# The exponentials of a softmax taken head by head from PSUM on ScalarE, in a kernel of attention, sampling and two recurrences

## What is computed

```python
xn = _rms_norm(x, g_norm) * (1.0 + scale) + shift
q, k, v = ...(xn @ W_qkv)                     # 16 heads, d = 32
q = _rms_norm(q, g_q)
k = _rms_norm(k, g_k)
logits = jnp.einsum('bhqd,bhkd->bhqk', q, k) * d ** (-0.5)
attn = jax.nn.softmax(logits, axis=-1)
o = jnp.einsum('bhqk,bhkd->bhqd', attn, v)
x = x + o + o @ W_out
```

## Time and profile before

| | |
|---|---|
| median of 3 runs | 1828.99 us (1824.32 to 1829.84) |
| profiled execution | 1831.36 us, span 1829.4 us |
| TensorE, matmuls, busy | 1593.6 us (87%) |
| VectorE busy | 1582.0 us (86%) |
| ScalarE busy | 821.4 us (45%) |
| GpSimd busy | 697.0 us (38%) |
| mean granted clock of TensorE | 0.967 |

### The profile page before, as it was taken

The page is one execution under the profiler, slowest core; times in us unless marked ns, Lnnn a source line. Parts: engine busy times, 40 slices in busy tenths (PEclk is TensorE's granted clock), DMA queues, the critical chain, the costliest instruction groups (busy, mean ns, idle before and its releaser), DMA issues.

```text
span 1829.4 us, 100329 instructions
## 1 busy us (share of the span) xinstructions
PE 1593.6 (87%) x44506; PEld 1398.0 (76%) x44506; DVE 1582.0 (86%) x3935; ACT 821.4 (45%) x1886; POOL 697.0 (38%) x832
## 2 busy tenths in 40 slices
PE   5778778788878787885799999999999999999995
PEld 4355555556555555555799999999999999999995
DVE  5699999999999999986289888888988988899887
ACT  3533333323333333333255555555555555555553
POOL 2333333333333333334433444434443344434342
PEclk9889999999999999997799999999999999999999
DMA  5200010000000000002000000000000000000000
GB/s 183 93 16 23 25 25 18 24 23 25 26 25 17 25 23 26 20 13 80 6 10 14 13 14 16 14 13 14 13 15 15 13 13 15 15 14 13 14 15 15
DMA packets 91905, 45.47 MB, mean 25 GB/s; under 512 B 75984, under 2 KB 84240, under 8 KB 91472
## 3 DMA queue, kind: packets, MB, share of 16 engines
q1 hardware_dynamic: 91024, 39.03, 8.9%
q0 software_dynamic: 448, 0.02, 0.1%
HBM read 30.56 MB, written 8.45 MB: 21 GB/s over the span
## 4 chain that ended last, share of the span: by engine, by line
PE 49%; DVE 1%; issue 1%; POOL 0%; ACT 0%; POOLq 0%; ACTq 0%; DVEq 0%
PE ps_RZ L1032 20%; PE ps_F L1059 13%; PE ps_N L1032 10%; PE ps_F L1064 6%; DVE ps_S L1199 0%; DVE rest L1199 0%; DVE ts L1224 0%; DVE cub L1228 0%; ACT ps_T L1096 0%; POOL en L1337 0%; DVE ps_E L1199 0%; DVE qst L1199 0%; DVE Qs L1323 0%; DVE Hf L1220 0%; DVE P L1316 0%
## 5 line engine op out<-in xcount | busy, mean ns | idle before, releaser
L1059 PE MATMUL ps_F<-ts,Cp 128*128 128x64 f16 x8192 | 283.2, 193 | 12.7 <-ACT ts L1096 11.5
L825 PE MATMUL psQ<-Wx,front 128*128 128x512 f16 x1152 | 285.6, 401 | 1.2 <-issue 1.2
L1059 PEld LDWEIGHTS ps_F<-ts,Cp 128*128 128x128 f16 x8192 | 257.5, 98 | 14.6 <-ACT ts L1096 12.4
L634 DVE TENSOR_SCALAR E<-rows,lidx 128x512 f16<-128x512 f16 x512 | 229.4, 500 | 0.0
L1096 ACT ACTIVATE ts<-qst 128x256 f16<-128x256 f32 x192 | 80.1, 417 | 311.1 <-DVE qst L1199 311.1
L825 PEld LDWEIGHTS psQ<-Wx,front 128*128 128x128 f16 x1152 | 115.7, 103 | 133.7 <-issue 29.6
L1032 PE MATMUL ps_RZ<-xs,Wx 128*128 128x64 f16 x6144 | 204.0, 194 | 3.8 <-POOL xs L1341 2.4
L1032 PE MATMUL ps_RZ<-hs,Whh 128*128 128x64 f16 x6144 | 201.6, 193 | 1.3 <-POOL hs L1337 0.4
L1032 PEld LDWEIGHTS ps_RZ<-xs,Wx 128*128 128x128 f16 x6144 | 191.0, 99 | 5.5 <-POOL xs L1341 2.9
L1032 PEld LDWEIGHTS ps_RZ<-hs,Whh 128*128 128x128 f16 x6144 | 188.5, 98 | 2.4 <-issue 1.6
L1064 PE MATMUL ps_F<-ts,Cp 128*128 128x64 f16 x4096 | 163.0, 193 | 1.0 <-issue 0.3
(11 more groups left out here) (167 smaller groups left out, 3515.3 us busy)
## 6 DMA issues: line engine op xcount, KB each, us to landing
front<-in_x SPq DMA_DIRECT2D x32, 256.0 KB, 3.6
rows<-rows_dram SPq DMA_DIRECT2D x64, 128.0 KB, 3.0
out<-ot SPq DMA_DIRECT2D x512, 16.0 KB, 1.8
XR<-in_L_cond_W_qkv SPq DMA_DIRECT2D x4, 768.0 KB, 16.3
E<-in_L_cond_W_hh SPq DMA_DIRECT2D x4, 768.0 KB, 4.4
front<-in_L_cond_W_ih SPq DMA_DIRECT2D x4, 768.0 KB, 5.8
XR<-in_L_cond_W_emb SPq DMA_DIRECT2D x1, 2048.0 KB, 11.0
E<-in_L_cond_coupling SPq DMA_DIRECT2D x1, 1024.0 KB, 5.5
```

The lines of the kernel that those rows point to most:

```text
L634: e = v.tensor_scalar(E[b][:, t, c, :], rows[b][:, :], lidx[:, t, c:c + 1], None, ALU.is_equal)
L825: last = mm(psQ[:, n, :], xn[p.u][:, i, c, :], Wqkv[:, j, c, n * D:(n + 1) * D], start=(c == 0 and t == 0), stop=(c == KC - 1 and t == 2))
L1059: mm(psF[:, s % 2, m, :], Cp[:, i, c, m * PART:(m + 1) * PART], ts_[:, 0, c, :], start=(c == 0 and m == 0 and i == 0), stop=False, skip_gr ...
```

## The change

`subtract_max` becomes `least`: VectorE takes the minimum of each head (`mn`) straight from the scores, which now carry the opposite sign, as `gqk` is negated. ScalarE computes exp(-score + minimum) from `psS` for each of the 16 heads in an instruction of its own, with the minimum as bias and the sum over the head written to `den` by `accum_out`. `sum_p` becomes `invert_sum`, the reciprocal alone. The waits of `turn_qk`, `scores` and `turn_x` for `sub_done` become waits for `exp_done`.

```diff
-        v.tensor_scalar(gqk[:, :], gq[:, 0:1], gq[:, 1:2], float(DH) ** -0.5, ALU.mult, ALU.mult)
+        v.tensor_scalar(gqk[:, :], gq[:, 0:1], gq[:, 1:2], -float(DH) ** -0.5, ALU.mult, ALU.mult)
...
         def exps(p):
-            act.wait_ge(sub_done, p.n + 1)
-            a(S[:, :, :], S[:, :, :], ACT.Exp).then_inc(exp_done, 1)
+            act.wait_ge(mn_done, p.n + 1)
+            need(act, p_T, p.n)
+            need(act, rden_done, p.n)
+            for c in range(4):
+                for r in range(4):
+                    h = c * 4 + r
+                    last = a(S[:, h, :], psS[:, r, c * T:(c + 1) * T], ACT.Exp, scale=-1.0, bias=mn[:, r, c:c + 1],
+                             accum_out=den[:, h:h + 1])
+            last.then_inc(exp_done, 1)
...
-        def subtract_max(p):
-            sc = psS[:, :, 0:256].rearrange("p r (c k) -> p r c k", c=4)
+        def least(p):
             dve.wait_ge(sc_done, p.n + 1)
-            v.tensor_reduce(mx[:, :, :], sc, AX.X, ALU.max).then_inc(mx_done, 1)
-            dve.wait_ge(mx_done, p.n + 1)
-            need(dve, p_T, p.n)
-            v.tensor_tensor(S[:, :, :].rearrange("p (c r) k -> p r c k", r=4), sc,
-                            mx[:, :, :].unsqueeze(3).broadcast_to([PART, 4, 4, T]), ALU.subtract).then_inc(sub_done, 1)
+            need(dve, exp_done, p.n)
+            v.tensor_reduce(mn[:, :, :], psS[:, :, 0:256].rearrange("p r (c k) -> p r c k", c=4), AX.X, ALU.min).then_inc(mn_done, 1)
...
-        def sum_p(p):
+        def invert_sum(p):
             dve.wait_ge(exp_done, p.n + 1)
-            v.tensor_reduce(den[:, :], S[:, :, :], AX.X, ALU.add).then_inc(den_done, 1)
-            dve.wait_ge(den_done, p.n + 1)
             need(dve, p_done, p.n)
             v.reciprocal(rden[:, :], den[:, :]).then_inc(rden_done, 1)
...
         def turn_x(p):
             pe.wait_ge(y_done, p.n + 1)
             pe.wait_ge(x_in[p.u], p.half * 16 + 16)
-            need(pe, sub_done, p.n - 2)
+            need(pe, exp_done, p.n - 2)
```

More of the change, by code:

```diff
@@ L298, in attention_and_sampling @@
     S = sb("S", [PART, HEADS, T])
-    mx = sb("mx", [PART, 4, 4])
+    mn = sb("mn", [PART, 4, 4])
     den = sb("den", [PART, HEADS])
@@ L331, in attention_and_sampling @@
     qk_T, qk_hi, qk_ready = sem("qk_T"), sem("qk_hi"), sem("qk_ready")
-    sc_done, mx_done, sub_done, exp_done = sem("sc_done"), sem("mx_done"), sem("sub_done"), sem("exp_done")
-    den_done, rden_done, p_done = sem("den_done"), sem("rden_done"), sem("p_done")
+    sc_done, mn_done, exp_done = sem("sc_done"), sem("mn_done"), sem("exp_done")
+    rden_done, p_done = sem("rden_done"), sem("p_done")
     p_T, pt_hi, pt_ready = sem("p_T"), sem("pt_hi"), sem("pt_ready")
@@ L764, in slot @@
             if p := pair(-1):
-                subtract_max(p)
+                least(p)
             if tap:
@@ L768, in slot @@
             if p := pair(-1):
-                sum_p(p)
+                invert_sum(p)
             if tap:
@@ L799, in turn_qk @@
             pe.wait_ge(qn_done, p.n * 2 + 2)
-            need(pe, sub_done, p.n)
+            need(pe, exp_done, p.n)
             need(pe, pt_ready, p.n)
```

## The result

The changed kernel takes 1874.5 us (median of 4 runs, 1869.5 to 1879.7) against 1827.4 for the kernel before: ratio 1.026, 95% interval 1.0225 to 1.0292. It is slower by 47 us; 62 were forecast. Its profiled execution has a span of 1877.9 us, 48.5 more than that of before.

A forecast was written before the change was run, and what follows sets the result against it. VectorE was taken to bound the attention and sampling slots, TensorE the recurrences. Longer slots (46.8 + 3.9 = 50.7 us) plus clock falls (11.5) gave 62.2 us on the 1829.0 median: 1891 us, range 1855 to 1940.

The forecast's parts named there:

- Who sets the slot: VectorE in the attention and sampling slots: almost no slack, so its path from maximum to second tap product sets their length.
- The price of a head: ScalarE's sixteen exponentials: 0.31 us a head for ACTIVATE and accumulator read, 5.08 us in all in place of 1.06.
- Rival A: ScalarE's accumulator reads run in series: 0.42 to 0.53 us a head, kernel about 1932 to 1990 us; chance 0.2.
- rival B: Small ScalarE instructions overlap fully: 0.12 us a head, about 1784 us; chance 0.04 faster, 0.03 time unchanged near 0.22.
- The segment: VectorE from reduction to second tap product: 5.02 to 6.53 us, 1.51 more a slot, 46.8 us over 31 slots.
- The slot of pair 0: Slot in which nothing is sampled or projected out: the delay of `turn_x` lacks cover, costing 3.9 us instead of 1.5.
- The clock: TensorE idles longer before `turn_p`, so its granted clock falls in ten more slots, 1.15 us each: 11.5 us.
- The total: Whole kernel: 50.7 us of longer slots plus 11.5 us of clock falls, 62.2 us slower; chance of slower 0.92.

## Why the prediction was right, and where its sizes were off

*Who sets the slot.* Right. VectorE's order from the reduction to the second tap product is the slot: 5.02 to 6.29 us there, 24.66 to 25.92 us in the slot. That the wait and not ScalarE's load is the loss is shown by the new order: -122 us with the same instructions, of which VectorE's idle time is the larger part (83 of the 104 us over 24 slots).

*The price of a head.* 0.31 us were forecast from rows of 512 elements, 0.29 measured; the sixteen 4.85 instead of 5.08 us. The rows gave the pointer as 0.099 and the read as 0.10; taken away one by one they are 0.094 and 0.09. Rival A (reads in series, 0.42 and more) and B (full overlap, 0.12) are both excluded. The pitch of 0.22 us at which rival B was to decide doesn't go with its 3.57 us for all: by the prediction's own 15 pitches and the 0.43 of the last pair it is 0.21.

*The segment.* 1.27 us more a slot, 1.51 forecast: 0.23 by the heads. Over the 30 slots behind that of pair 0 up to the last reduction this is 38 us, where the sum has 46.8 for 31; it is the largest part of the miss.

*The slot of pair 0.* +5.0, forecast 3.9. `turn_x` is released by the exponentials and the projection behind it ran at the lower clock:

```profile
80.16 1.94 PE L914 MATMUL psS<-ident,front 128*128 128x128 f32 x8 [9.56 <-issue]
...
81.89 4.88 PE L826 MATMUL psQ<-Wx,front 128*128 128x512 f16 x12
...
86.81 0.60 ACT L486 ACTIVATE front<-psQ 128x512 f32<-128x512 f32 x1 [0.83 <-PE psQ L826]
```

In the earlier trace rows ScalarE was ready for the squares only at 84.99 because of its copies; now it waits for TensorE.

*The clock.* Size right (13.6 us, 11.5 forecast; 12 more long slots, ten forecast; 1.15 us each), its ground wrong. The forecast had `turn_x` all but unmoved and the gap in front of `turn_p` longer by 1.5 us. That gap stayed (2.47 us on average before, 2.35 after). The 0.3 us were taken from the slot of the earlier trace rows, in which `turn_x` starts 6.0 us after the reduction; in 20 of the 27 slots it starts 4.4 to 5.1 us after, as in the slot from 373.99 (378.62). Moved to 6.3 us it opens a new gap of up to 1.6 us, and `project(p, 0)` behind it moves as well, which is why the gap in front of `turn_p` doesn't grow. So TensorE's waits in a slot did grow by about 1 us (from 2.5 to (51.6 + 23.9) / 22 = 3.4), but in another place. That idle time brings on the falls is shown by the filled kernels for the gap in front of `turn_p`. That the place matters little is shown by the run without the sum: there `turn_x` starts 4.8 us after the reduction again in most slots, all the waiting is in front of `turn_p` (3.61 us in its timeline, 75.2 us in 22 slots), and 21 of 27 slots are long, where the changed kernel has 75.5 us in two gaps and 22 long slots. Filling the new gap alone was not tried.

*The total.* 62 us forecast, 56 in the same parts of the span (38 + 5 + 13.6), 47 by the medians. The other 8 us between the profiled executions lie ahead of and behind the slots, where runs differ by about as much without the change.

## What to carry to other kernels

Splitting one wide ScalarE instruction by head pays its fixed part sixteen times: here 0.09 us for each pointer operand and 0.09 for each accumulator read, on a path in which the bounding engine waits. Work taken off the bounding engine counts only if that engine has something to do meanwhile: ask what it will wait for, and move independent work in front of the wait; the same change went from +2.6% to -4.1% by that, where the new order alone took 2.3% off the kernel before. A gain by reordering is not explained until the busy and the idle time of the bounding engine are compared: here contention looked like the reason, and it had only moved. Compute idle gaps from an ordinary slot, not from the one at hand.

## What the runs showed of the hardware

- Within the sixteen heads the rows of ScalarE grow from 0.31 to 0.40 us (ACTIVATE) and from 0.20 to 0.29 (read), while the starts stay 0.29 us apart. The duration of a row does not give the rate; the distance of the starts does.
- Six useless matmuls a slot, 1.46 us by their row, made the kernel before faster by 0.6%: of 27 slots, those with a granted clock partly at 1.2 GHz went from twelve to five, and those five were no longer than the others (24.65 us).
- The same 512-wide tap matrix takes 0.26 us when VectorE is ahead of GpSimd's scaling, and 0.59 on average of eight when it is behind. Moving it ahead left VectorE's busy time of 24 slots as it was (551.6 and 553.9 us), since other tap matrices then stood beside GpSimd.
